# First half of the value projection moved from key tile 7 to key tile 6 in a fused attention kernel

## The chip, the cores and the metric

The kernel runs on one NeuronCore of a Trainium2 chip. The metric is the device time of one execution in microseconds (us); lower is better. Engines are named as in the profile: PE (TensorE matmuls), PEld (TensorE weight loads), DVE (VectorE), ACT (ScalarE), POOL (GpSimd), SP (SyncE, which issues all DMAs here).

## The reference, cut to what matters

One transformer block on x of shape (4, 1024, 256): self attention with 16 heads of 64, cross attention to a context of 77 rows, and a feed-forward layer, each behind a layer norm whose gain and shift come from a condition vector. The change lies in the self attention:

```python
def _attn(xq, ctx, wq, wkv, wo, bo):
    q = _heads(xq @ wq)
    k, v = jnp.split(ctx @ wkv, 2, axis=-1)
    ...
    sim = jnp.einsum('bhnd,bhmd->bhnm', q, k) * DH ** (-0.5)
    a = jax.nn.softmax(sim, axis=-1)
    o = jnp.einsum('bhnm,bhmd->bhnd', a, v)
    ...
    return o @ wo + bo
attn_in = _adaln(x, cond, ln1_w, ln1_b, g1_w, g1_b, b1_w, b1_b)
x = _attn(attn_in, attn_in, sa_wq, sa_wkv, sa_wo, sa_bo) + x
```

## The kernel before, in words

The self attention (`self_attention`) works through 32 head pairs: 4 batches times 8 pairs of heads, counted by g from 0 to G - 1 = 31. The 1024 keys of a pair are cut into 8 key tiles (kt) of 128. The 1024 queries are handled in two halves (c = 0 and 1), and the two heads of a pair lie in the two halves of the 128 partitions. Products of 16-bit high and low parts stand in for 32-bit ones, so each projection has three terms.

The order of the work on every engine is written out by hand: each engine has its own loop over g and kt, and semaphores join them. Engines work strictly in that order. In step (g, kt) PE does, in turn:

- `differences(j, kt)` (L460) for the next pair j = g + 1, into `ps_t`, whose halves are the two turning buffers `turn[0]` and `turn[1]`. ACT's `rises` (L701) takes the positive part of it.
- `scores(g, kt, c)` (L483), twelve matmuls into `ps_s[0]` and `ps_s[1]`. For kt = 0 the order is c = 1, then c = 0, and c = 0 also waits for the evacuated values (`s_v_r`).
- `bases(j, kt)` (L467), again into `ps_t`, after ACT's rise. DVE's `maxima` (L895) then writes one column of row maxima per head to `mx`.
- `shift()` (L490), which subtracts the row maxima in `m_line` from the scores. For kt = 0 it waits for the DMA that brings that line (`s_line`). ACT's `exponentials` (L713) follow, one for each c.
- `values(g, kt - 1, 0)` (L505), an extra piece of work if the step has one, and `values(g, kt - 1, 1)`.

The extra pieces are hung on certain key tiles, and those on the turning buffers have to wait until DVE has read the maxima there (`maxima_free`). K projections of pair g + 2 stand in key tiles 0 and 1, Q projections of pair g + 3 in 3 and 5 (L55, evacuated by ACT at L687), and the second half of the value projection (`V_SECOND`, L43, evacuated at L692) in key tile 2. The column sums of the previous pair (`totals`, L515, evacuated at L732) stand in key tile 0. Every projection into a turning buffer is followed, at the head of the next step, by a wait for its evacuation.

At the end of key tile 7 stands the turn to the next pair: PE transposes `mx` into `turn[1]` (L660), waits for the exponential of c = 0, and computes the first half of the value projection of pair j into the left half of `ps_s[0]` (`project_v(j, 0)`, L43). Meanwhile ACT copies the transposed maxima to `m_rows` (`row`, L705) and SP sends them to `m_line` by DMA (L302). Then ACT evacuates the values (`evacuate_v`, L692). The next step, key tile 0 of the next pair, opens with waits, the last of which is this one, because `differences` overwrites `turn[1]`:

```python
if kt == 0:
    pe.wait_ge(s_kd, j + 1)
    ...
    pe.wait_ge(s_mt_r, g + 1)
```

Some pairs carry more. For each of the six later layer norms (`NORMS`, with the pair it begins in), ACT normalises rows (`normalise`, L745) in key tiles 4 to 7 of the pair after the first and 0 to 3 of the one after that. In the second and third pair after the first, PE transposes the normalised rows (`transposes`, L540) in key tiles 4 and 6 (`NORM_AT`), ACT scales them (`norm_affine`, L752) and rounds them (`norm_high`, L757), and DVE makes the low half (`norm_low`, L982). In pairs 9, 17 and 25 (`late_norm`) PE writes the eight output row tiles of the batch that is done (`output`, L524 and L55; `Y_AT`), and DVE adds the residual (L928). DVE further sums the exponentials (`add_probs`, L908) in every step and makes the low half of the keys (`low`, L887), in key tile 7 for the K side of pair g + 2.

Of the kernel before, what the change touches and what calls it, by code (L numbers as in the profile page):

```python
# [14 lines left out]
B, N, D = 4, 1024, 256  # L15
# [44 lines left out]
def self_attention(nc, consts, x_src, x_dst, cond, norm, weights, bo, xT, wq, wk, wv, wo, shared, context, following):  # L60
# [9 lines left out]
    K_AT, Q_AT = (0, 1), (3, 5)  # L70
    V_FIRST, V_SECOND = NK - 1, 2
    Y_AT = {1: (0,), 2: (1,), 3: (2,), 4: (3, 4), 5: (5,), 6: (6, 7)}
    NORMS = {1: (0, 1), 2: (5, 2), 3: (10, 3), 4: (16, 0), 5: (21, 1), 6: (28, 2)}
    CROSS_NORMS = 4
    NORM_AT = {(2, 4): 0, (2, 6): 1, (3, 4): 2, (3, 6): 3}
    STATS_AT = {0: (0, 1, 2), 1: (3,), 3: (4, 5), 5: (6, 7)}
    STEPS = 10
    with ExitStack() as ctx:
# [153 lines left out]
        def v_bank(j, c):  # L232
            return turn[0] if c or j == 0 else ps_s[0][:, 0:HALF]

# [37 lines left out]
        def y_bank(b, t):  # L272
            if b < B - 1:
                return turn[0 if t in (3, 6) else 1][:, 0:D]
            places = [ps_s[0][:, 0:D], ps_s[0][:, HALF:HALF + D], ps_s[1][:, 0:D], ps_s[1][:, HALF:HALF + D],
                      turn[0][:, 0:D], turn[1][:, 0:D], ps_o[:, 0:D], ps_o[:, HALF:HALF + D]]
            return places[t]
# [5 lines left out]
        def score_count(g, kt, c):  # L283
            return 2 * NK * g + 2 * kt + order(kt).index(c) + 1
# [153 lines left out]
        def _(pe):  # L438
# [149 lines left out]
            for g in range(G):  # L588
                j = g + 1
                for kt in range(NK):  # L590
                    if j < G:
                        if kt == 0:
                            pe.wait_ge(s_kd, j + 1)
                            pe.wait_ge(s_hi[0], j + 1)
                            pe.wait_ge(s_hi[1], j + 1)
                            pe.wait_ge(s_mt_r, g + 1)
                            if g == 0:
                                pe.wait_ge(s_v_r, 1)
                        else:
                            maxima_free(j, kt - 1, 2)  # L600
                            if kt - 1 in K_AT and g + 2 < G:
                                pe.wait_ge(s_kq_r[0], 2 * (g + 2) + K_AT.index(kt - 1) + 1)
                            if kt - 1 in Q_AT and g + 3 < G:
                                pe.wait_ge(s_kq_r[1], 2 * (g + 3) + Q_AT.index(kt - 1) + 1)
                            if kt - 1 == V_SECOND and g >= 0:
                                pe.wait_ge(s_v_r, 2 * g + 2)
                            if kt == 1 and g >= 1:
                                pe.wait_ge(s_sum_r, g)
                            if norm_bank(g, kt - 1) is not None:
                                u, n = norm_bank(g, kt - 1)  # L610
                                pe.wait_ge(s_nxn, 4 * u + n + 1)
                            for b, t in y_tiles(g, kt - 1):
                                pe.wait_ge(s_yr, TT * b + t + 1)
                        differences(j, kt)
# [13 lines left out]
                    if last[0] >= 0:  # L628
                        values(*last, 0)
                    if j < G and (kt in K_AT + Q_AT + (V_SECOND,) or norm_bank(g, kt) is not None):  # L630
                        maxima_free(j, kt, 1)
# [4 lines left out]
                    if kt == V_SECOND and g >= 0:  # L636
                        project_v(g, 1)
                    if norm_bank(g, kt) is not None:
                        u, n = norm_bank(g, kt)
# [16 lines left out]
                    if last[0] >= 0:  # L656
                        values(*last, 1)
                    if kt == V_FIRST and j < G:
                        maxima_free(j, kt, 2)
                        pe.transpose(turn[1][0:2 * TT, 0:P], mx[:, j % 2, :], ident[:, :]).then_inc(s_mt, 1)  # L660
                        pe.wait_ge(s_p, score_count(g, kt, 0))
                        project_v(j, 0)
            for c in range(2):
# [18 lines left out]
        def _(act):  # L682
# [121 lines left out]
            for g in range(G):  # L804
                j = g + 1
                for kt in range(NK):
# [27 lines left out]
                    if kt == V_SECOND and g >= 0:  # L834
                        evacuate_v(g, 1)
                    if kt == 0 and g >= 1:
                        evacuate_sums(g - 1)
                        evacuate_o(g - 1, 1)
# [8 lines left out]
                    if norm_bank(g, kt) is not None:  # L847
                        norm_affine(*norm_bank(g, kt))
                        norm_high(*norm_bank(g, kt))
                    if kt == V_FIRST and j < G:  # L850
                        row(j)
                        evacuate_v(j, 0)
                    if g == G - 2 and kt in (1, 3):
# [16 lines left out]
        def _(dve):  # L870
# [205 lines left out]
            for g in range(G):  # L1076
                j = g + 1
                for kt in range(NK):
                    if j < G:
                        maxima(j, kt)  # L1080
                    if kt == 6 and norm_bank(g, 4) is not None:
                        norm_low(*norm_bank(g, 4))
# [29 lines left out]
                    if kt == 6 and g >= 1 and not late_norm(g):  # L1112
                        low_output(g - 1, 0)
                    if kt == 7 and g + 2 < G:
                        low(g + 2, 0)
# [11 lines left out]
                    if norm_of(g, 1) is not None and kt == 3:  # L1127
                        newton_step(norm_of(g, 1))
                    if kt == 0 and g >= 1 and norm_bank(g - 1, 6) is not None:
                        norm_low(*norm_bank(g - 1, 6))  # L1130
                    if g == G - 2 and kt in (2, 4):
# [1175 lines left out]
```

## Time and profile before

| what | us |
|---|---|
| runs | 2149.64, 2154.3, 2148.78; median 2149.64 |
| the profiled execution, its own time | 2151.02 |
| its span from first to last instruction | 2149.2 |
| mean granted TensorE clock, share of full speed | 0.981 |

A timeline lists instructions in order of time with their start, length, engine, source line and tiles; neighbours of a kind are merged into one line with a count. In brackets stands how long the engine was idle before it, and what ended that. Matmuls are pipelined: the length shown for one is longer than the distance to the next.

### The profile page before, as it was taken

Reading aid. Unit: us, or ns where it says so; the run is one execution under the profiler, and the core shown is the slowest. Engines: PE = TensorE matmul, PEld = TensorE weight load, DVE = VectorE, ACT = ScalarE, POOL = GpSimd, SP = SyncE. Lnnn points to the kernel's source line nnn. Section 1 sums busy time; section 2 is a strip of 40 time slices with the busy share of each in tenths; the row PEclk is TensorE's granted clock in tenths of the full one; section 3 lists DMA queues with packets and bytes.
Section 4 is the critical chain, followed back from the end, with each engine's and each line's share of the span. In section 5 each row is a group of like instructions: output and inputs, shape, how many; then the busy total and the mean of one; then the engine's idle time right before and its main releaser. Section 6 shows DMA issues by size and latency. Waiting matters only on the chain. (4 is left out here: it accounts for less than half of the span.)

```text
span 2149.2 us, 43063 instructions
## 1 busy us (share of the span) xinstructions
PE 2040.5 (95%) x17544; PEld 934.3 (43%) x17544; DVE 1751.1 (81%) x2720; ACT 1429.1 (66%) x1844; POOL 18.1 (1%) x16
## 2 busy tenths in 40 slices
PE   4799999999999999999999999999988999979999
PEld 2233333345333334533333453333633455446676
DVE  6899899986999998699989779987588888754754
ACT  4588778774787777577787657786457666652452
POOL 3000000000000000000000000000000000000000
PEclk8899999999999999999999999999998999999999
DMA  6010111011111111111011012021332344333111
GB/s 204 30 40 31 60 40 41 31 60 41 61 41 40 51 41 41 41 60 60 31 41 41 31 51 80 31 56 35 102 113 91 106 145 141 105 101 109 40 40 40
DMA packets 100347, 136.62 MB, mean 64 GB/s; under 512 B 34533, under 2 KB 73399, under 8 KB 100151
## 3 DMA queue, kind: packets, MB, share of 16 engines
q1 hardware_dynamic: 100151, 133.88, 18.9%
q8 instruction: 139, 2.28, 0.4%
q14 instruction: 57, 0.47, 0.1%
HBM read 68.34 MB, written 13.11 MB: 38 GB/s over the span
## 5 line engine op out<-in xcount | busy, mean ns | idle before, releaser
L713 ACT ACTIVATE sa_probs<-sa_ps_s 128x1024 f32<-128x1024 f32 x512 | 496.1, 1022 | 130.9 <-PE sa_ps_s L490 130.8
L505 PE MATMUL sa_ps_o<-sa_probs,sa_v_pair 128*64 128x512 f32 x2048 | 531.0, 609 | 1.4 <-DVE sa_mx L895 1.4
L908 DVE TENSOR_TENSOR sa_acc<-sa_acc,sa_probs 128x1024 f32<-128x1024 f32 x384 | 452.7, 1220 | 19.8 <-ACT sa_probs L713 11.9
L895 DVE CUSTOM_DVE_ANT_0 sa_rise<-sa_ps_t,sa_rise 128x512 f32<-128x512 f32 x504 | 327.3, 687 | 121.8 <-PE sa_ps_t L467 121.6
L483 PE MATMUL sa_ps_s<-scores_or_weights 64*128 64x512 f16 x3072 | 374.8, 376 | 1.5 <-ACT raw_or_keys L687 1.5
L701 ACT ACTIVATE sa_rise<-sa_ps_t 128x1024 f32<-128x1024 f32 x252 | 257.4, 1021 | 140.8 <-PE sa_ps_t L460 139.4
L483 PEld LDWEIGHTS sa_ps_s<-scores_or_weights 64*128 64x128 f16 x3072 | 151.9, 94 | 156.1 <-ACT sa_v_pair L692 6.8
L505 PEld LDWEIGHTS sa_ps_o<-sa_probs,sa_v_pair 128*64 128x64 f32 x2048 | 115.8, 135 | 149.8 <-issue 126.8
L460 PE MATMUL sa_ps_t<-sa_kd,scores_or_weights 64*128 64x512 f16 x504 | 99.3, 389 | 19.3 <-ACT scores_or_weights L697 6.8
L460 PEld LDWEIGHTS sa_ps_t<-sa_kd,scores_or_weights 64*128 64x128 f16 x504 | 25.2, 93 | 201.1 <-issue 163.1
L467 PE MATMUL sa_ps_t<-scores_or_weights 64*128 64x512 f16 x504 | 98.1, 385 | 11.3 <-ACT sa_rise L701 11.2
L490 PE MATMUL sa_ps_s<-sa_m_line,sa_m_ones 32*128 32x512 f16 x1024 | 101.3, 385 | 0.0
L687 ACT ACTIVATE raw_or_keys<-sa_ps_t 128x512 f32<-128x512 f32 x118 | 71.1, 603 | 32.6 <-PE sa_ps_t L55 32.6
L908 DVE TENSOR_TENSOR sa_acc<-sa_probs 128x1024 f32<-128x1024 f32 x64 | 75.5, 1221 | 9.1 <-ACT sa_probs L713 6.4
L873 DVE TENSOR_TENSOR raw_or_keys<-raw_or_keys,ropeC 128x1024 f32<-128x1024 f32 x64 | 78.0, 1219 | 5.3 <-DMA sa_swp<-raw_or_keys 5.3
L55 PE MATMUL ca_ps_t<-xT_hi,scores_or_weights 128*64 128x512 f16 x512 | 80.6, 396 | 0.0
L2113 ACT ACTIVATE ff_hid<-ff_ps_h,ff_b_col 128x1024 f32<-128x1024 f32 x32 | 35.6, 1113 | 62.3 <-PE ff_ps_h L43 61.4
L878 DVE TENSOR_TENSOR raw_or_keys<-raw_or_keys,sa_swp 128x1024 f32<-128x1024 f32 x62 | 75.7, 1221 | 1.1
L874 DVE TENSOR_TENSOR sa_swp<-sa_swp,ropeS 128x1024 f32<-128x1024 f32 x62 | 75.5, 1218 | 0.0
L55 PE MATMUL ca_ps_t<-scores_or_weights,ca_o_hi 128*64 128x256 f16 x800 | 74.7, 284 | 0.0
L887 DVE TENSOR_TENSOR scores_or_weights<-raw_or_keys,scores_or_weights 128x1024 f16<-128x1024 f32 x62 | 73.8, 1191 | 0.4 <-ACT scores_or_weights L697 0.4
L697 ACT ACTIVATE scores_or_weights<-raw_or_keys 128x1024 f16<-128x1024 f32 x64 | 67.4, 1054 | 9.8 <-DVE raw_or_keys L878 9.8
(338 smaller groups left out, 3656.2 us busy)
## 6 DMA issues: line engine op xcount, KB each, us to landing
sa_swp<-raw_or_keys SPq DMA_DIRECT2D x124, 256.0 KB, 2.4
sa_inv<-sa_scratch SPq DMA_DIRECT2D x128, 128.0 KB, 2.9
ca_swp<-raw_or_keys SPq DMA_DIRECT2D x64, 256.0 KB, 2.4
ca_inv<-ca_scratch SPq DMA_DIRECT2D x64, 256.0 KB, 3.9
sa_xs<-in_x SPq DMA_DIRECT2D x4, 1024.0 KB, 5.7
sa_xr<-in_x SPq DMA_DIRECT2D x4, 1024.0 KB, 6.8
x_after_cross<-scores_or_weights SPq DMA_DIRECT2D x32, 128.0 KB, 2.2
ff_xr<-x_after_cross SPq DMA_DIRECT2D x4, 1024.0 KB, 6.3
```

The source lines that it names most:

```text
L55: ins = pe.matmul(out[part], lhs[a][lhs_at(k)][:, part], rhs[b][rhs_at(k)], start=(start and i == 0), stop=(stop and i == len(terms) - 1))
L460: ins = pe.matmul(max_banks(j, t)[:, half(x)], hi[rows(x), j % 3, 1, t * P:(t + 1) * P], kd[rows(x), j % 2, :], start=True, stop=True)
L467: ins = pe.matmul(max_banks(j, t)[:, half(x)], hi[rows(x), j % 3, 1, t * P:(t + 1) * P], hi[rows(x), j % 3, 0, 0:HALF], start=True, stop=True)
L483: pe.matmul(ps_s[c][:, half(x)], k[rows(x), s, 0, ks], q[rows(x), s, 1, half(c)], start=(n == 0), stop=False)
L490: ins = pe.matmul(ps_s[c][:, half(x)], m_ones[quarter, :], m_line[quarter, :], start=False, stop=True)
L505: ins = pe.matmul(ps_o[rows(x), half(c)], v_pair[:, kt, rows(x)], probs[:, kt % 2, c, half(x)], start=(kt == 0), stop=(kt == NK - 1))
L701: act.activation(rise_of(j, t), max_banks(j, t), ACT.Relu).then_inc(s_rise, 1)
L713: act.activation(probs[:, kt % 2, c, :], ps_s[c][:, :], ACT.Exp, scale=float(DH) ** -0.5).then_inc(s_p, 1)
L873: dve.tensor_tensor(raw[:, i, :], raw[:, i, :], ropeC[:, :], ALU.mult).then_inc(s_mul[i], 1)
L878: dve.tensor_tensor(raw[:, i, :], raw[:, i, :], swapped(j, i)[:, :], ALU.add).then_inc(s_rot[i], 1)
L895: dve.tensor_tensor_reduce(out=larger, in0=max_banks(j, t)[:, half(x)], in1=larger, scale=1.0, scalar=-3.0e38, op0=ALU.add, op1=ALU.max, a ...
L908: dve.tensor_tensor(acc[:, c, :], before, probs[:, kt % 2, c, :], ALU.add).then_inc(s_acc[c], 1)
```

## The change

The first half of the value projection moves from the end of key tile 7 to key tile 6, between the two `values` of that step, and goes to `turn[0]` in place of `ps_s[0]`; ACT evacuates it there, and PE waits for that at the head of key tile 7. The transpose of the maxima stays at the end of key tile 7, as do `row` and its DMA. What stood on `turn[0]` in key tile 6 makes room: the second and fourth of each layer norm's transposes go to key tile 7, the last output row tile goes to key tile 7, and the buffers of output tiles 6 and 7 change places. At the head of the next key tile 0, PE now also waits for the evacuation of those two. On DVE, the low half of the K side goes from key tile 7 to 6, and a layer norm's low half from key tile 6 to 5.

```diff
-    V_FIRST, V_SECOND = NK - 1, 2
-    Y_AT = {1: (0,), 2: (1,), 3: (2,), 4: (3, 4), 5: (5,), 6: (6, 7)}
+    V_FIRST, V_SECOND = NK - 2, 2
+    Y_AT = {1: (0,), 2: (1,), 3: (2,), 4: (3, 4), 5: (5,), 6: (6,), 7: (7,)}
...
-    NORM_AT = {(2, 4): 0, (2, 6): 1, (3, 4): 2, (3, 6): 3}
+    NORM_AT = {(2, 4): 0, (2, 7): 1, (3, 4): 2, (3, 7): 3}
...
         def v_bank(j, c):
-            return turn[0] if c or j == 0 else ps_s[0][:, 0:HALF]
+            return turn[0]
...
-                return turn[0 if t in (3, 6) else 1][:, 0:D]
+                return turn[0 if t in (3, 7) else 1][:, 0:D]
...
                             pe.wait_ge(s_mt_r, g + 1)
+                            if norm_bank(g - 1, NK - 1) is not None:
+                                u, n = norm_bank(g - 1, NK - 1)
+                                pe.wait_ge(s_nxn, 4 * u + n + 1)
+                            for b, t in y_tiles(g - 1, NK - 1):
+                                pe.wait_ge(s_yr, TT * b + t + 1)
...
+                            if kt - 1 == V_FIRST:
+                                pe.wait_ge(s_v_r, 2 * j + 1)
...
-                    if j < G and (kt in K_AT + Q_AT + (V_SECOND,) or norm_bank(g, kt) is not None):
+                    if j < G and (kt in K_AT + Q_AT + (V_FIRST, V_SECOND) or norm_bank(g, kt) is not None):
                         maxima_free(j, kt, 1)
...
+                    if kt == V_FIRST and j < G:
+                        project_v(j, 0)
...
-                    if kt == V_FIRST and j < G:
+                    if kt == NK - 1 and j < G:
                         maxima_free(j, kt, 2)
                         pe.transpose(turn[1][0:2 * TT, 0:P], mx[:, j % 2, :], ident[:, :]).then_inc(s_mt, 1)
-                        pe.wait_ge(s_p, score_count(g, kt, 0))
-                        project_v(j, 0)
...
+                    if kt == V_FIRST and j < G:
+                        evacuate_v(j, 0)
...
-                    if kt == V_FIRST and j < G:
+                    if kt == NK - 1 and j < G:
                         row(j)
-                        evacuate_v(j, 0)
...
-                    if kt == 6 and norm_bank(g, 4) is not None:
+                    if kt == 5 and norm_bank(g, 4) is not None:
                         norm_low(*norm_bank(g, 4))
...
-                    if kt == 7 and g + 2 < G:
+                    if kt == 6 and g + 2 < G:
                         low(g + 2, 0)
...
-                    if kt == 0 and g >= 1 and norm_bank(g - 1, 6) is not None:
-                        norm_low(*norm_bank(g - 1, 6))
+                    if kt == 0 and g >= 1 and norm_bank(g - 1, 7) is not None:
+                        norm_low(*norm_bank(g - 1, 7))
```

## Rows read from the trace of the kernel before

**Rows 1.** The page, part 1: busy us, share of the span, instructions of each engine.
```profile
PE 2040.5 (95%) x17544; PEld 934.3 (43%) x17544; DVE 1751.1 (81%) x2720; ACT 1429.1 (66%) x1844; POOL 18.1 (1%) x16
```

**Rows 2.** Windows from one `differences` to the next: stretch, us, busy us per engine, clock, DMA.
```profile
780.98:785.01 4.03, 4.03 (x30) 1.28 (x29) 3.65 (x8) 3.29 (x4) 0.00 (x0) 1.00 0.34 136
785.01:790.59 5.58, 5.58 (x56) 2.72 (x55) 5.58 (x9) 3.94 (x6) 0.00 (x0) 1.00 0.00 0
...
760.68:766.31 5.63, 5.63 (x55) 2.54 (x54) 5.23 (x10) 3.56 (x4) 0.00 (x0) 1.00 0.37 140
```

**Rows 3.** Timeline of PE, key tile 7 of a plain pair and the next key tile 0.
```profile
786.53 0.38 PE L467 MATMUL sa_ps_t<-scores_or_weights 64*128 64x512 f16 x2
...
789.04 0.28 PE L660 MATMUL sa_ps_t<-sa_ident,sa_mx 128*16 128x128 f32 x1
...
792.26 0.39 PE L467 MATMUL sa_ps_t<-scores_or_weights 64*128 64x512 f16 x2
792.58 0.40 PE L490 MATMUL sa_ps_s<-sa_m_line,sa_m_ones 32*128 32x512 f16 x4
```

**Rows 4.** Timeline of ACT, the same pair, key tiles 2 and 7.
```profile
765.40 0.60 ACT L692 ACTIVATE sa_v_pair<-sa_ps_t 128x512 f32<-128x512 f32 x1 [0.50 <-PE sa_ps_t L43]
...
787.29 1.94 ACT L713 ACTIVATE sa_probs<-sa_ps_s 128x1024 f32<-128x1024 f32 x2 [0.31 <-PE sa_ps_s L490]
789.35 0.27 ACT L705 ACTIVATE sa_m_rows<-sa_ps_t 16x128 f16<-16x128 f32 x1
790.69 0.60 ACT L692 ACTIVATE sa_v_pair<-sa_ps_s 128x512 f32<-128x512 f32 x1 [1.07 <-PE sa_ps_s L43]
```

**Rows 5.** The waits of the whole span: us in total, times, longest us.
```profile
PEld sa_ps_s L483 <- ACT sa_v_pair L692: 6.8, 31, 0.4
```

**Rows 6.** Timeline of PE and ACT, layer norm pair with normalisation in key tile 7.
```profile
612.27 0.39 PE L460 MATMUL sa_ps_t<-sa_kd,scores_or_weights 64*128 64x512 f16 x2
...
616.43 0.28 PE L660 MATMUL sa_ps_t<-sa_ident,sa_mx 128*16 128x128 f32 x1
...
617.98 0.39 PE L460 MATMUL sa_ps_t<-sa_kd,scores_or_weights 64*128 64x512 f16 x2
...
617.00 0.25 ACT L705 ACTIVATE sa_m_rows<-sa_ps_t 16x128 f16<-16x128 f32 x1
```

**Rows 7.** Timeline of PE and ACT, key tile 6 of a pair with layer norm transposes.
```profile
651.89 0.39 PE L460 MATMUL sa_ps_t<-sa_kd,scores_or_weights 64*128 64x512 f16 x2
...
656.92 0.39 PE L460 MATMUL sa_ps_t<-sa_kd,scores_or_weights 64*128 64x512 f16 x2 [0.20 <-ACT sa_xn L752]
...
655.99 0.78 ACT L752 ACTIVATE sa_xn<-sa_ps_t,bet,gam 128x512 f32<-128x512 f32 x1
656.81 0.63 ACT L757 ACTIVATE xT_hi<-sa_xn 128x512 f16<-128x512 f32 x1
657.35 1.02 ACT L701 ACTIVATE sa_rise<-sa_ps_t 128x1024 f32<-128x1024 f32 x1
```

**Rows 8.** Timeline of PE, key tile 6 of pair 9: starts of output row tiles.
```profile
520.74 0.30 PE L524 MATMUL sa_ps_t<-sa_bo_rows,sa_two_ones 128*64 128x256 f16 x2
...
523.49 0.28 PE L524 MATMUL sa_ps_t<-sa_bo_rows,sa_two_ones 128*64 128x256 f16 x2
```

**Rows 9.** Timeline of DVE, the plain pair, from key tile 7 into key tile 0.
```profile
790.69 1.22 DVE L887 TENSOR_TENSOR scores_or_weights<-raw_or_keys,scores_or_weights 128x1024 f16<-128x1024 f32 x1
...
792.69 0.69 DVE L895 CUSTOM_DVE_ANT_0 sa_rise<-sa_ps_t,sa_rise 128x512 f32<-128x512 f32 x1 [0.18 <-PE sa_ps_t L467]
```

**Rows 10.** DMA issues (count, KB each, median us to landing), and SP's timeline at that turn.
```profile
sa_swp<-raw_or_keys SPq DMA_DIRECT2D x124, 256.0 KB, 2.4
...
sa_few<-sa_sums SPq DMA_DIRECT2D x128, 2.0 KB, 1.8
...
sa_m_line<-sa_m_rows SPq DMA_DIRECT2D x32, 4.0 KB
...
789.64 0.62 SPq L302 DMA_DIRECT2D sa_m_line<-sa_m_rows  x1
```

## The prediction

> **What bounds the kernel now.** I began with the page's busy shares: PE shows 95%, DVE 81%, ACT 66% [rows 1]. Then I read the timeline of PE and cut it into steps, from one `differences` to the next, because the change only moves work between the steps of key tiles 6, 7 and 0. The windows over these steps show the pattern [rows 2]. A step of a plain pair without an extra piece (key tile 6) takes 4.03 us. The step of key tile 7 with the turn to the next pair takes 5.58. Key tile 2, which carries the other half of the same value projection, takes 5.63. PE is busy from end to end in all three. I take the length of a step, not the busy share, as the measure of what PE's order costs, since every piece hung on a step lengthens it.
>
> The second thing to see is what lies at the turn. The transpose of the maxima starts at 789.04 [rows 3]. ACT's copy of it starts at 789.35, when that 0.28 us transpose is through, and ends at 789.62 [rows 4]. ACT's two exponentials had ended before (787.29 + 1.94 = 789.23), so they do not set this. The next `differences` starts only at 790.59 [rows 2], because PE is in the value projection until then. The wait for ACT's copy (`s_mt_r`) is therefore already over when PE gets to it. The projection costs PE time there, but it also covers that chain.
>
> **The change part by part.** I count one plain pair first, then the others. All sums are against the profiled execution.
>
> Key tile 6 gains the projection. The nearest row is key tile 2, which has the same 24 matmuls, the same buffer and the same place between two `values`: 5.63 against 4.03, so +1.60 [rows 2]. The lower end is what the projection costs at the turn: 790.59 - 789.04 = 1.55 with the maxima's transpose in it [rows 2, 3], so about 1.40 without. I take 1.60, the same place. ACT's evacuation (0.60) now stands in key tile 6 ahead of ACT's rise of key tile 7, and PE waits for it before that step's `differences`. In key tile 2 the same evacuation ends at 766.00, and `differences` starts at 766.31 [rows 2, 4]. It is hidden by `values`, with 0.3 to spare; without that cover the step would be up to 0.6 longer.
>
> Key tile 7 loses the projection, and now nothing stands between the transpose and the wait. From the transpose's start, ACT's copy ends 789.62 - 789.04 = 0.58 later. PE's reaction comes on top. Where PE's `differences` waited for ACT in the same place, ACT ended at 655.99 + 0.78 = 656.77 and PE went on at 656.92 [rows 7], so 0.15; I take that, with 0 as the lower end. The step up to the transpose is 789.04 - 785.01 = 4.03 [rows 2, 3]. The new step is 4.03 + 0.58 + 0.15 = 4.76, against 5.58: -0.82.
>
> Key tile 0 loses a small stall. Its scores for c = 0 waited for the values, 31 times and 6.8 us in all [rows 5], and ACT's rise stood behind the evacuation. From `differences` to `bases` it took 792.26 - 790.59 = 1.67, where the step before took 786.53 - 785.01 = 1.52 [rows 2, 3]: -0.15. The lower end of this gain is 0.
>
> A plain pair: 1.60 - 0.82 - 0.15 = **+0.63**.
>
> In a pair with normalisation in key tile 7, that work stands ahead of ACT's copy. The copy ends at 617.25, 0.82 after the transpose [rows 6]. The new step is 4.03 + 0.82 + 0.15 = 5.00 against 617.98 - 612.27 = 5.71, so the pair is 1.60 - 0.71 - 0.15 = +0.74. I take 4.03 up to the transpose, although it shows 4.16 now, because the evacuation pushes the normalisation before it out of the rise's way.
>
> In a pair with layer norm transposes, key tile 6 is 656.92 - 651.89 = 5.03 now [rows 7], and becomes 5.63. In key tile 7, ACT does `norm_affine` and `norm_high` between the exponentials and the copy. In key tile 6 the next ACT instruction comes at 657.35, which is 5.46 after the step's start [rows 7]. Adding the copy and PE's reaction gives 5.46 + 0.27 + 0.15 = 5.88 against 5.58. The pair is 0.60 + 0.30 - 0.15 = +0.75.
>
> In the pairs with output rows, one row tile costs 523.49 - 520.74 = 2.75 [rows 8] in either step, so moving it changes nothing: +0.63 as in a plain pair. Its residual on DVE is hidden by the second `values`.
>
> By the code's tables, of the 31 turns 12 are plain, 3 have output rows, 5 normalisation in key tile 7, and 11 transposes. The sum is 15 x 0.63 + 5 x 0.74 + 11 x 0.75 = 9.5 + 3.7 + 8.3 = +21.4 us.
>
> Moved at no cost: the low half of the keys on DVE. It takes 1.22 [rows 9]. DVE is busy 3.65 in key tile 6, so 4.87 there in a step of 5.63 [rows 2]. Behind it stand the maxima of key tile 7, which PE needs only at the transpose. DVE's wait of 0.18 at 792.69 [rows 9] shows that it keeps up with the turn now, and it has 1.22 less to do there afterwards. Without that cover it would add what it is late by, at most 1.22. The layer norm's low half only goes one step forward within DVE's order. In the last pair, the transposes in key tile 7 stand beside the wait for the last column sums. SP and POOL issue nothing new; SP's DMA of the maxima stands behind the same copy.
>
> That DMA loses cover, though. The copy ends at 789.62, the DMA is issued at 789.64 [rows 10], and `shift` of key tile 0 needs it at 792.58 [rows 3], so 2.96 after the copy. After the change, `shift` follows the copy by 0.15 + 1.52 + (792.58 - 792.26) = 1.99. The trace gives no landing time for this DMA of 4 KB. The nearest row, 2 KB from the same memory, lands after 1.8, the 256 KB ones after 2.4 [rows 10]. With 1.8 and PE's reaction it is ready at 0.02 + 1.8 + 0.15 = 1.97, just hidden, and I take 0. The ends are 0, as it cannot gain, and 2.96 - 1.99 = 0.97 a turn, as no row shows PE waiting for it now.
>
> The Trainium skill (DMA: Bandwidth & Descriptors, Anatomy of one DMA) puts a fixed 2.0 us on a DMA of any size. By that, `shift` would wait (0.02 + 2.0 + 0.15) - 1.99 = 0.18 a turn, and the sum would be an estimated 5.6 us more. No row here shows this DMA's landing, and the 1.8 beside it is lower, so I stay with the row.
>
> **Against the runs.** The profiled execution took 2151.02, which is its span of 2149.2 and 1.8 around it. The median of the three runs is 2149.64, 1.4 lower. The forecast goes from the median: 2149.64 + 21.4 = **2171.0 us**, +1.0%. A measurement of this kernel can tell about 0.3%, 6.4 us, from no change.
>
> **The rivals.** (a) The copy is hidden after all, and the step of key tile 7 shrinks by all that the projection took there, 5.58 to about 4.15. Then a turn costs 1.60 - 1.43 - 0.15 = 0.02, and the time is 2150. Against it, the transpose (0.28) and the copy (0.27) run one after the other, with nothing of PE beside them. Chance 6%.
>
> (b) Faster: PE is not the limit in key tile 6, and the projection disappears in its gaps. It decides where key tile 6 grows by less than the 0.82 + 0.15 = 0.97 that the turn gives back. If it were fully hidden, the time would be 2149.64 - 31 x 0.97 = 2120. For it speaks that weight loads fill only 43% [rows 1]; against it that the same projection lengthened key tile 2 by 1.60. Chance 5%. The Trainium skill (Perfetto Trace Analysis, Identifying the Most-Contended Engine) says that a matmul's busy share misjudges PE and that the share of weight loads is to be used. That is this rival, and the step lengths here speak against it.
>
> (c) Slower still: the line of maxima lands late, as the larger DMAs do. With 2.4, `shift` waits 0.02 + 2.4 + 0.15 - 1.99 = 0.58 a turn, 18 us more, 2189. It decides from 1.84 us of landing time. For it speaks how little is to spare, against it the 1.8. Chance 9%.
>
> That the change does not do what it says could show only in the freed bank: the scores of key tile 0 still begin with c = 1, so the freed `ps_s[0]` brings nothing but the 0.15.
>
> **How the numbers follow.** The forecast has 80%. Its low end: projection at 1.40 (-6), PE's reaction at 0 (-5); not both in full, so -10. Its high end: no gain in key tile 0 (+5) and the line late by a little (+6), so about +10. The range is 2161 to 2181; 6% and 5% lie below it with (a) and (b), most of (c) above. Slower by over 0.3%: the forecast less a small tail, and (c), 87%. Within 0.3%: (a) and that tail, 8%. Faster: 5%.
>
> **What would show it.** In the profile after, key tile 6 of a plain pair should take about 5.6, key tile 7 about 4.8, with the idle time of 0.5 to 0.6 before `differences` of key tile 0 put down to ACT's copy, and key tile 0 about 6.5. A turn with transposes should show ACT's `norm_high` ahead of the copy. It would be wrong if key tile 7 ends right behind the transpose, if key tile 6 grows by less than 1, or if PE waits at `shift` for the line.

## The result and the profile after

The change made the kernel slower by 49 us: 2199.53 us, median of four runs (2199.1 to 2204.81), against 2150.26, median of four (2148.78 to 2154.3). The ratio is 1.0233, with a 95% interval of 1.0215 to 1.0251. The direction is the forecast one, the size is not: 2171.0 was forecast, and the range ended at 2181.

The profiled execution is the slowest of the four, 2204.81, of which the span is 2202.9. Part of the growth of the span lies in the first pair, at the start of the kernel. That pair took between 45.9 and 49.2 us in the traces of this study (45.97 before, 49.23 after, 46.54 in a kernel that differs from the one after only in SP's order), and I leave its length out of the sums. The page, part 1, of the kernel after:

```profile
PE 2054.7 (93%) x17544; PEld 939.4 (43%) x17544; DVE 1753.0 (80%) x2720; ACT 1433.0 (65%) x1844; POOL 18.1 (1%) x16
```

PE's share fell from 95% to 93% [rows 1]. In microseconds, its busy time grew by only 14 (2054.7 - 2040.5) while the span grew by 53.7. So most of the loss is time in which PE waits; the 14 come up again with the clock below. The windows of the kernel after, from one `differences` to the next, tell where. The first three are key tiles 6, 7 and 0 of a plain turn, the last two key tile 7 of pair 9, which has output rows, and the key tile 0 behind it.

```profile
805.76:811.39 5.63, 5.63 (x55) 2.54 (x54) 5.25 (x10) 4.08 (x5) 0.00 (x0) 1.00 0.25 98
811.39:816.14 4.75, 4.30 (x31) 1.40 (x30) 4.53 (x9) 3.75 (x5) 0.00 (x0) 1.00 0.00 0
816.14:822.61 6.47, 6.47 (x48) 2.22 (x48) 6.04 (x9) 4.54 (x6) 0.00 (x0) 1.00 0.00 1
538.36:549.62 11.26, 7.22 (x82) 4.00 (x80) 4.96 (x9) 4.13 (x6) 0.00 (x0) 0.92 0.01 2
549.62:560.58 10.96, 10.07 (x48) 3.08 (x49) 6.85 (x12) 4.71 (x6) 0.00 (x0) 0.62 0.28 96
```

Against [rows 2], the plain turn does what was forecast: key tile 6 went from 4.03 to 5.63 and key tile 7 from 5.58 to 4.75. The turn of pair 9 does not. Its key tiles 7 and 0 took 5.58 and 6.64 before, and now take 11.26 and 10.96, at a mean granted clock of 0.62 in the second.

Cutting both traces at every `differences` gives the length of each pair. I worked these out from the starts of L460; each pair runs from its key tile 1 to the next key tile 0:

| kind of pair | before | after | difference | forecast |
|---|---|---|---|---|
| plain (12) | 42.03 | 42.64 | +0.61 | +0.63 |
| normalisation in key tile 7 (5) | 43.19 | 43.91 | +0.72 | +0.74 |
| layer norm transposes (11) | 44.52, 44.03 | 45.34, 44.85 | +0.82 | +0.75 |
| the same, pairs 3, 8, 19: more in key tile 0 | 6.63 | 8.61, 8.04, 7.99 instead of 6.47 | +2.14, +1.57, +1.52 | 0 |
| output rows, pairs 9, 17, 25 | 64.49, 64.50, 64.50 | 73.07, 71.19, 73.62 | +8.58, +6.69, +9.12 | +0.63 each |

Three pairs are counted with their kinds although their own lengths differ: pair 0 (plain) for the reason given, pair 29 (normalisation) with 41.23 and 42.05, and pair 30 (transposes), which has no next `differences` to end it.

The first three kinds make 7.3 + 3.6 + 9.0 = 19.9 us, the extra of pairs 3, 8 and 19 makes 5.2, and the pairs with output rows 24.4. That is 49.5, against 49.3 measured; the medians are not known to 0.2, so that part of the agreement is luck. Almost all that was missed lies in six turns.

The waits of PE in the kernel after (us in total, times, longest us) name three causes that the kernel before does not have at these places:

```profile
PE sa_ps_t L460 <- ACT sa_m_rows L712: 18.1, 27, 1.0
PE sa_ps_t L460 <- DVE sa_xr L936: 11.9, 3, 4.0
PE sa_ps_s L490 <- DMA sa_m_line<-sa_m_rows: 9.1, 7, 2.1
```

**The first** is the forecast one. The timeline of a plain turn, of PE and then of ACT:

```profile
815.42 0.28 PE L669 MATMUL sa_ps_t<-sa_ident,sa_mx 128*16 128x128 f32 x1
816.14 0.39 PE L460 MATMUL sa_ps_t<-sa_kd,scores_or_weights 64*128 64x512 f16 x2 [0.45 <-ACT sa_m_rows L712]
816.36 1.47 PE L483 MATMUL sa_ps_s<-scores_or_weights 64*128 64x512 f16 x12
...
815.73 0.27 ACT L712 ACTIVATE sa_m_rows<-sa_ps_t 16x128 f16<-16x128 f32 x1
```

ACT's copy ends at 816.00, 0.58 after the transpose began, and PE goes on 0.14 later. The working had 0.58 and 0.15.

**The second** belongs to the three pairs with output rows. The turn of pair 9, in the order PE, ACT, DVE, SP:

```profile
544.31 0.28 PE L55 MATMUL sa_ps_t<-sa_wo_lo,sa_o_hi 128*64 128x256 f16 x2
...
545.38 0.28 PE L669 MATMUL sa_ps_t<-sa_ident,sa_mx 128*16 128x128 f32 x1
549.62 0.61 PE L460 MATMUL sa_ps_t<-sa_kd,scores_or_weights 64*128 64x512 f16 x2 [3.97 <-DVE sa_xr L936]
550.00 2.79 PE L483 MATMUL sa_ps_s<-scores_or_weights 64*128 64x512 f16 x12
...
554.11 0.61 PE L490 MATMUL sa_ps_s<-sa_m_line,sa_m_ones 32*128 32x512 f16 x4 [0.89 <-DMA sa_m_line<-sa_m_rows]
...
544.69 1.15 ACT L733 ACTIVATE sa_o_hi<-sa_o_pair 128x512 f16<-128x512 f32 x2 [4.88 <-PE sa_ps_t L55]
545.74 1.92 ACT L720 ACTIVATE sa_probs<-sa_ps_s 128x1024 f32<-128x1024 f32 x2
547.55 0.25 ACT L712 ACTIVATE sa_m_rows<-sa_ps_t 16x128 f16<-16x128 f32 x1
...
546.78 2.36 DVE L916 TENSOR_TENSOR sa_acc<-sa_acc,sa_probs 128x1024 f32<-128x1024 f32 x2 [5.17 <-ACT sa_probs L720]
549.06 0.42 DVE L936 SCALAR_TENSOR_TENSOR sa_xr<-sa_ps_t,sa_xr 128x256 f32<-128x256 f32 x1
...
549.50 0.38 SPq L387 DMA_DIRECT2D x_after_self<-sa_xr  x1
549.92 0.62 SPq L302 DMA_DIRECT2D sa_m_line<-sa_m_rows  x1
```

Start at ACT. Its `high_output` (L733) rounds the output of the pair just done into `o_hi`, and the row tiles of the batch still read `o_hi`. In these pairs it therefore waits until all eight row tiles are through PE. The eighth was moved to key tile 7, so ACT stands still for 4.88 us until 544.69. Behind it in ACT's order stand the exponentials of key tile 7. DVE's sums need those, DVE's residual (L936) stands behind the sums in DVE's order, and it ends at 549.48. PE waits for it, because the row tile lies in the turning buffer: 3.97 us idle. Afterwards PE's twelve `scores` matmuls take 2.79 where a plain turn has 1.47.

The granted clock is the reason for that. It has two levels in these traces, 1.00 (2.4 GHz) and 0.50 (1.2 GHz), and 0.62 is a mean of both. While PE stands idle it falls to 0.50, and it stays there for the first 8.3 us of key tile 0. The windows of that stretch, and of the key tiles 0 behind pairs 17 and 25:

```profile
549.62:557.95 8.33, 7.44 (x32) 2.61 (x34) 5.71 (x9) 3.52 (x4) 0.00 (x0) 0.50 0.37 126
927.37:936.44 9.07, 7.83 (x48) 2.65 (x50) 5.86 (x9) 4.54 (x6) 0.00 (x0) 0.85 0.35 118
1309.73:1321.24 11.51, 10.58 (x48) 3.15 (x49) 5.87 (x9) 4.72 (x6) 0.00 (x0) 0.59 0.27 91
```

PE is busy for 10.07, 7.83 and 10.58 us in these three steps, where a plain key tile 0 has 6.47. The lower clock thus takes 9.1 us of the 24.4, most of the 14 by which PE's busy time grew. The wait ahead was 3.97 all three times, but the lower level ended sooner behind pair 17, which is why that pair lost about 2 us less than the other two.

**The third** lies on SP's queue. When all rows of a batch are done, SP stores 1 MB (L387); it waits for the residual of the eighth tile, so it is now issued at 549.50, just ahead of the line of maxima at 549.92. At the turn after pair 3, it is a load that stands there (L333). It waits until PE has done the transposes of the layer norm before, and the last set of these was moved to key tile 7 as well. SP, then PE, of the kernel after:

```profile
255.84 0.39 SPq L333 DMA_DIRECT2D sa_xs<-in_x  x1
257.71 0.62 SPq L302 DMA_DIRECT2D sa_m_line<-sa_m_rows  x1
...
257.94 0.39 PE L460 MATMUL sa_ps_t<-sa_kd,scores_or_weights 64*128 64x512 f16 x2 [0.92 <-ACT sa_m_rows L712]
...
261.92 0.39 PE L490 MATMUL sa_ps_s<-sa_m_line,sa_m_ones 32*128 32x512 f16 x4 [2.07 <-DMA sa_m_line<-sa_m_rows]
```

SP in the kernel before, at the same two places:

```profile
245.73 0.39 SPq L333 DMA_DIRECT2D sa_xs<-in_x  x1
251.54 0.62 SPq L302 DMA_DIRECT2D sa_m_line<-sa_m_rows  x1
...
526.88 0.38 SPq L387 DMA_DIRECT2D x_after_self<-sa_xr  x1
531.81 0.62 SPq L302 DMA_DIRECT2D sa_m_line<-sa_m_rows  x1
```

There, the large transfer has 4.9 to 5.8 us before the small one is issued. After the change it has 0.4 to 1.9. The line of 4 KB then reaches PE 261.92 - 257.71 = 4.21 us after its issue.

### The profile page after: what moved, and what is told of

Read it like the earlier page. It is cut to its first block and busy times, and to the rows that moved or that the text cites. A ratio compares the mean times of both kernels' runs of the same rounds, so it can differ in the third digit from the quotient of the medians.

```text
span 2202.9 us, 43080 instructions
## 1 busy us (share of the span) xinstructions
PE 2054.7 (93%) x17544; PEld 939.4 (43%) x17544; DVE 1753.0 (80%) x2720; ACT 1433.0 (65%) x1844; POOL 18.1 (1%) x16
## 5 line engine op out<-in xcount | busy, mean ns | idle before, releaser
L505 PE MATMUL sa_ps_o<-sa_probs,sa_v_pair 128*64 128x512 f32 x2048 | 540.3, 613 | 1.4 <-DVE sa_mx L903 1.4
L460 PE MATMUL sa_ps_t<-sa_kd,scores_or_weights 64*128 64x512 f16 x504 | 100.0, 391 | 47.2 <-ACT sa_m_rows L712 18.1
L460 PEld LDWEIGHTS sa_ps_t<-sa_kd,scores_or_weights 64*128 64x128 f16 x504 | 25.7, 93 | 230.9 <-issue 210.1
L43 PE MATMUL sa_ps_t<-sa_wv_hi,xT_hi 128*128 128x128 f16 x512 | 90.9, 222 | 0.9 <-DVE sa_mx L903 0.9
L43 PE MATMUL sa_ps_t<-sa_wv_hi,xT_lo 128*128 128x128 f16 x512 | 90.2, 220 | 0.0
L43 PE MATMUL sa_ps_t<-sa_wv_lo,xT_hi 128*128 128x128 f16 x512 | 90.2, 220 | 0.0
```

The lines of the kernel that those rows point to most:

```text
L43: ins = pe.matmul(out, lhs[a][lhs_at(k)], rhs[b][rhs_at(k)], start=(start and i == 0), stop=(stop and i == len(terms) - 1))
L460: ins = pe.matmul(max_banks(j, t)[:, half(x)], hi[rows(x), j % 3, 1, t * P:(t + 1) * P], kd[rows(x), j % 2, :], start=True, stop=True)
L505: ins = pe.matmul(ps_o[rows(x), half(c)], v_pair[:, kt, rows(x)], probs[:, kt % 2, c, half(x)], start=(kt == 0), stop=(kt == NK - 1))
```

## The experiments

The theory was that three costs add up: the turn (about 20 us), ACT's wait for the eighth row tile (with the lower clock behind it), and the line behind the large transfer. The rival was that the row tiles and transposes are harmless, and that the projection in key tile 6 itself delays ACT and DVE in those turns.

**The line first.** The kernel after, with SP's issue of the line ahead of the store and the load:

```diff
+                if g + 1 < G:
+                    line(g + 1)
                 if g >= PAIRS and g % PAIRS == 1:
...
                     load_norm(norm_of(g, -2))
-                if g + 1 < G:
-                    line(g + 1)
```

> The change with one edit: SP issues the DMA of the maxima line ahead of the store of finished output rows and the load for the next layer norm, instead of behind them. Queue theory (a 1 MB transfer moved just ahead of that small DMA makes it land after 3.6 to 4.2 us instead of 1.7): the stalls at shift of key tile 0 after pairs 3, 8 and 19 (2.1 + 1.6 + 1.5) and the one in the three pairs with output rows go, together about 9 us, 2190 us against 2199.5. Rival (the excess comes from DVE's moved low halves or from the TensorE clock alone): no change, 2199.

Measured: 2186.52, ratio to the kernel before 1.0167 (1.0147 to 1.0186). The windows of pair 9's key tile 7 and of the key tile 0 behind it, then PE's wait for the line:

```profile
532.21:543.47 11.26, 7.22 (x82) 4.00 (x80) 4.95 (x9) 4.13 (x6) 0.00 (x0) 0.91 0.01 3
543.47:552.23 8.76, 8.76 (x48) 2.72 (x48) 6.14 (x11) 4.65 (x6) 0.00 (x0) 0.72 0.35 120
```
```profile
PE sa_ps_s L490 <- DMA sa_m_line<-sa_m_rows: 1.0, 1, 1.0
```

The waits for the line fell from 9.1 to 1.0 us, and key tile 0 after pairs 3, 8 and 19 is back at 6.47: the order on SP's queue was the cause there. The 1.0 that is left stands at the last turn, where no `differences` come ahead of `shift`. Key tile 7 of pair 9 is unchanged, with its wait for DVE's residual. Its key tile 0 is still 8.76 with PE busy throughout, where a plain one takes 6.47. With no wait left in it, these 2.3 us go with the clock: it stands at 0.50 for the first 4.9 us of the step, and half of that is 2.4.

**The rounding late.** The kernel after, with ACT's `high_output` behind the exponentials in those pairs:

```diff
-                    if kt == 7 and g >= 1:
-                        if late_norm(g):
-                            high_output(g - 1, 0)
+                    if kt == 7 and g >= 1 and not late_norm(g):
                         high_output(g - 1, 1)
                     if g >= 0:
                         for c in order(kt):
                             exponentials(g, kt, c)
+                    if kt == 7 and g >= 1 and late_norm(g):
+                        for c in range(2):
+                            high_output(g - 1, c)
```

> The change with one edit: in the pairs with output rows ACT rounds the finished outputs of the previous pair (which waits for the last output row tile) behind the exponentials of key tile 7 instead of ahead of them. Chain theory (last row tile, rounding, exponentials, sums of exponentials, residual, then PE): key tile 7 of pairs 9, 17 and 25 falls from 11.26 to about 7.9, and PE's clock stays up in the next key tile 0, but the maxima line still stands behind the store; about 15 us off, 2184. Rival (the extra time of these pairs is the output tile's own cost or the store): 2197 to 2199.

Measured: 2181.63, ratio 1.015 (1.0125 to 1.0175). The same two windows, then PE's wait for the line:

```profile
535.70:543.59 7.89, 7.22 (x81) 4.01 (x80) 5.80 (x10) 4.27 (x6) 0.00 (x0) 1.00 0.04 13
543.59:551.70 8.11, 6.54 (x48) 2.22 (x48) 6.19 (x11) 4.54 (x6) 0.00 (x0) 1.00 0.35 120
```
```profile
PE sa_ps_s L490 <- DMA sa_m_line<-sa_m_rows: 10.5, 8, 2.1
```

Key tile 7 falls from 11.26 to 7.89, and the clock stays at 1.00 in both windows: ACT's wait was the head of that chain. Key tile 0 keeps 8.11 - 6.47 = 1.64 of the line's wait.

**Both.** The two edits together.

> Both edits on top of the change. If the two theories hold and do not overlap with the turn, what is left is the turn alone: plain pairs 42.64, pairs with output rows 66 to 67, 2172 us, 22 us over the kernel before. Rival: over 2185.

Measured: 2173.85, ratio 1.0109 (1.009 to 1.0127). The same two windows:

```profile
533.99:541.88 7.89, 7.23 (x81) 4.01 (x80) 5.80 (x10) 4.27 (x6) 0.00 (x0) 1.00 0.01 3
541.88:548.36 6.48, 6.48 (x50) 2.21 (x50) 4.90 (x8) 4.54 (x6) 0.00 (x0) 1.00 0.48 162
```

Pairs 9, 17 and 25 take 65.21, 65.70 and 65.21, so +0.7, +1.2 and +0.7 is left of +8.6, +6.7 and +9.1. All other pairs are as in the table, without the extra of pairs 3, 8 and 19. The sum by pairs, 19.9 + 2.6 = 22.5, meets the measured 2173.85 - 2151.45 = 22.4, closer than the four runs, which lie 5.5 apart, would let one expect. This is the cost that the forecast described.

With these kernels pair 9's +8.58 can be split: 0.72 with both edits, 11.26 - 7.89 = 3.37 for the chain in key tile 7, and 10.96 - 6.47 = 4.49 in key tile 0, of which 2.3 remains with the line first, and 2.2 goes with it. Only 0.89 of these 2.2 is PE's wait for the line; the rest goes with the lower clock, which lasted longer there. Over pairs 9, 17 and 25 together, the rounding late takes 17.4 us away, the line first 6.0, and both 21.8, so the costs do add up, nearly.

**The move without the rest.** The projection stays in key tile 6, but transposes and row tiles go back there, behind it, each with the wait that the shared buffer needs:

```diff
-    Y_AT = {1: (0,), 2: (1,), 3: (2,), 4: (3, 4), 5: (5,), 6: (6,), 7: (7,)}
+    Y_AT = {1: (0,), 2: (1,), 3: (2,), 4: (3, 4), 5: (5,), 6: (6, 7)}
...
-    NORM_AT = {(2, 4): 0, (2, 7): 1, (3, 4): 2, (3, 7): 3}
+    NORM_AT = {(2, 4): 0, (2, 6): 1, (3, 4): 2, (3, 6): 3}
...
-            return (ps_o[:, 0:HALF], ps_o[:, HALF:N], turn[0], turn[1])[n] if u == 0 else turn[0]
+            return (ps_o[:, 0:HALF], ps_o[:, HALF:N], turn[0], turn[1])[n] if u == 0 else turn[n % 2]
...
+                        if t == 7:
+                            pe.wait_ge(s_v_r, 2 * j + 1)
...
```

> The first half of the value projection in key tile 6 as in the change, but layer norm transposes and both last output row tiles stay in key tile 6 (the transposes in the other turning buffer, the last row tile behind the evacuation of the values). Turn theory: 31 turns at about 0.62 each and nothing else, 2170 us. Rival (moving the projection costs all of the 49 us, whatever stands beside it): 2199; rival (the moved tiles cost it all): 2150.

Measured: 2162.91, ratio 1.0061 (1.0044 to 1.0078), 7 us below what I expected, and far from both rivals. Key tile 6 of a pair with transposes:

```profile
658.37:664.50 6.13, 6.13 (x58) 2.94 (x57) 6.05 (x10) 4.86 (x7) 0.00 (x0) 1.00 0.23 88
```

Plain pairs still take 42.64, pairs 9, 17 and 25 64.80, 65.13 and 64.80. The pairs with transposes take 44.65 and 44.15, only +0.13. A set of transposes behind the projection adds 6.13 - 5.63 = 0.5, where in a key tile 6 of its own it added 5.03 - 4.03 = 1.0. That was not expected, and it is where most of the 7 us come from. Of the difference of 0.5, 0.20 is a wait: in the step of its own PE stands idle for 0.20 at the end, until ACT has evacuated the set [rows 7], and behind the projection it does not. The rest is open.

**The rest without the move.** The kernel before, with all other parts of the change (transposes and row tile in key tile 7, the low halves on DVE one step earlier), the projection at the turn:

```diff
-    Y_AT = {1: (0,), 2: (1,), 3: (2,), 4: (3, 4), 5: (5,), 6: (6, 7)}
+    Y_AT = {1: (0,), 2: (1,), 3: (2,), 4: (3, 4), 5: (5,), 6: (6,), 7: (7,)}
...
-    NORM_AT = {(2, 4): 0, (2, 6): 1, (3, 4): 2, (3, 6): 3}
+    NORM_AT = {(2, 4): 0, (2, 7): 1, (3, 4): 2, (3, 7): 3}
...
-                    if kt == 7 and g + 2 < G:
+                    if kt == 6 and g + 2 < G:
                         low(g + 2, 0)
...
```

> The kernel before with everything of the change but the projection: second and fourth layer norm transposes and the last output row tile in key tile 7, the low halves one key tile earlier, the projection still at the turn in the score buffer. Theory of three parts: no cost at plain turns (42.03 a pair); pairs 9, 17 and 25 still suffer the chain through the rounding and the late line, about 6 us each; the loads after pairs 3, 8 and 19 about 1 each: 2169 us. Rival (all cost hangs on the projection's place): 2150.

Measured: 2191.31, ratio 1.0175 (1.0154 to 1.0196), 22 us above what I expected. A wait of PE at the transpose of the maxima shows why:

```profile
PE sa_ps_t L665 <- DVE sa_mx L900: 10.3, 16, 1.1
```

DVE's low half, 1.22 us, now stands in a key tile 6 of 4.03 us with no projection to cover it, and the maxima come late. The next two kernels take this apart.

**The low half alone.** The kernel before, with only the last of these edits.

> The kernel before with one edit of the change: DVE makes the low half of the keys in key tile 6 instead of 7, and nothing else moves. Cover theory (this 1.2 us was free in the change only because the projection lengthened key tile 6): the maxima of key tile 7 come late, PE waits for them at their transpose, key tile 7 of a plain pair goes from 5.58 to about 6.24, as it did in e5_room_only, about 20 us in all, 2171 us. Rival (what lengthened e5_room_only's plain turns was something else in it): 2151.

Measured: 2162.6, ratio 1.005 (1.0033 to 1.0066). Key tile 7 of a plain pair, and PE's transpose of the maxima in it:

```profile
789.65:795.89 6.24, 5.65 (x56) 2.72 (x55) 6.24 (x10) 3.94 (x6) 0.00 (x0) 1.00 0.00 0
```
```profile
794.34 0.28 PE L660 MATMUL sa_ps_t<-sa_ident,sa_mx 128*16 128x128 f32 x1 [0.59 <-DVE sa_mx L895]
```

The step takes 6.24 instead of 5.58 (6.42 in some plain pairs), with DVE busy from end to end. The edit costs 11 us and not the 20 that I expected, because the pairs with transposes or row tiles have a longer key tile 6 here, which covers it: their key tile 7 takes 5.66 and 5.58.

**The tiles without the low half.** The kernel with the rest alone, the low half back in key tile 7:

```diff
-                    if kt == 6 and g + 2 < G:
+                    if kt == 7 and g + 2 < G:
                         low(g + 2, 0)
```

> e5_room_only with the low half of the keys back in key tile 7: the projection at the turn, the second and fourth layer norm transposes and the last output row tile in key tile 7. Plain turns back at 5.58; left are the chain and the late line in pairs 9, 17 and 25 and the loads after pairs 3, 8 and 19: 15 to 20 us over before, about 2170. Rival (the room costs nothing without the projection's move): 2151.

Measured: 2170.76, ratio 1.009 (1.0075 to 1.0105). Pair 9's key tile 7 and the key tile 0 behind it:

```profile
525.84:537.10 11.26, 8.74 (x105) 5.34 (x104) 4.15 (x8) 4.73 (x7) 0.00 (x0) 1.00 0.01 2
537.10:547.62 10.52, 7.89 (x48) 2.54 (x50) 7.90 (x13) 4.71 (x6) 0.00 (x0) 0.84 0.30 100
```

With the projection where it was, key tile 7 is again 11.26 long, and pairs 9, 17 and 25 take 71.33, 71.59 and 71.64. Key tile 0 after pairs 3, 8 and 19 takes 8.36, 7.64 and 7.76 instead of 6.63, while plain pairs take their 42.03. This decides against the rival: both missed costs come with the moved row tiles and transposes, and the projection need not move for them. The 19.0 here and the 10.8 of the low half alone make 29.8 of the 37.1 that the kernel with both lost. Most of the rest lies in the pairs with transposes: with both, their key tile 6 is short again and covers nothing, and their key tile 7 takes 7.22 against 6.31 here.

**Another bank for the maxima.** The kernel with both edits, and the transposed maxima in the freed bank `ps_s[0]`, so that only the scores of c = 0 wait for ACT's copy:

```diff
+        def row_bank(j):
+            return (ps_s[0] if j else turn[1])[0:2 * TT, 0:P]
...
                 elif c == 0:
                     pe.wait_ge(s_v_r, 2 * g + 1)
+                    pe.wait_ge(s_mt_r, g + 1)
...
-                            pe.wait_ge(s_mt_r, g + 1)
+                            if g == 0:
+                                pe.wait_ge(s_mt_r, g + 1)
...
+                        pe.wait_ge(s_p, score_count(g, kt, 0))
+                        pe.transpose(row_bank(j), mx[:, j % 2, :], ident[:, :]).then_inc(s_mt, 1)
...
```

> The change with both edits of e3_both, and the maxima are transposed into the score buffer that the projection has left, so that the differences of the next key tile 0 no longer wait for ACT's copy; only the scores of c = 0 do, which come 0.9 us later. Turn theory (the bare copy chain is what the turn costs): key tile 7 of a plain pair falls from 4.75 to about 4.15, 2150 us, level with the kernel before. Rival (the projection's place in key tile 6 is the cost, the wait only shows it): no change against e3_both.

Measured: 2164.93, ratio 1.0053 (1.0034 to 1.0071), where 2150 was expected. Key tile 7 and key tile 0 of a plain turn, PE's wait for the line, and that turn's timeline (ACT, SP, PE):

```profile
794.82:799.05 4.23, 4.23 (x31) 1.36 (x30) 4.01 (x8) 3.49 (x4) 0.00 (x0) 1.00 0.00 0
799.05:805.82 6.77, 6.54 (x51) 2.16 (x50) 6.74 (x11) 4.81 (x7) 0.00 (x0) 1.00 0.00 1
```
```profile
PE sa_ps_s L494 <- DMA sa_m_line<-sa_m_rows: 10.5, 31, 0.8
```
```profile
799.16 0.27 ACT L718 ACTIVATE sa_m_rows<-sa_ps_s 16x128 f16<-16x128 f32 x1
...
799.45 0.62 SPq L305 DMA_DIRECT2D sa_m_line<-sa_m_rows  x1
...
801.18 0.40 PE L494 MATMUL sa_ps_s<-sa_m_line,sa_m_ones 32*128 32x512 f16 x4 [0.23 <-DMA sa_m_line<-sa_m_rows]
```

Key tile 7 shrinks from 4.75 to 4.23, but key tile 0 grows from 6.47 to 6.77. With the wait for the copy gone, the next thing late is the line, at every one of the 31 turns. It reaches PE 801.18 - 799.45 = 1.73 us after its issue. So neither side came out: the wait for the copy did cost something, but only part of what its end saved is kept, because the next wait stands just behind it.

**Transposes beside other projections.** Since a set was cheap behind the value projection, I put all four sets of the kernel before behind projections in key tiles 5, 1, 3 and 5, in the other turning buffer and with the waits that this needs:

```diff
-    NORM_AT = {(2, 4): 0, (2, 6): 1, (3, 4): 2, (3, 6): 3}
+    NORM_AT = {(2, 5): 0, (3, 1): 1, (3, 3): 2, (3, 5): 3}
...
```

> The kernel before with the layer norm transposes hung on steps that already carry a projection (key tile 5 of one pair, 1, 3 and 5 of the next), in the other turning buffer. In e4_move_only a set of transposes behind the value projection lengthened its step by 0.5 us, alone in a step by 1.0. If that holds beside the K and Q projections too: 22 sets by 0.5, 11 us less than the kernel before, 2140. Rival (the 0.5 belongs to key tile 6, or DVE, which makes a low half more in these steps, comes late): 2151 or above.

Measured: 2151.35 (10 runs) against 2151.78 (13 runs), ratio 1.0002 (0.9992 to 1.0012): no difference, where 2140 was expected. Two of the steps that carry a set:

```profile
668.02:674.27 6.25, 6.25 (x47) 2.32 (x45) 4.52 (x9) 5.76 (x8) 0.00 (x0) 1.00 0.03 4
679.90:686.36 6.46, 6.26 (x46) 2.22 (x45) 6.46 (x10) 4.43 (x6) 0.00 (x0) 1.00 0.05 19
```

These are key tiles 1 and 3, which take 5.49 and 5.32 without a set: it costs 0.76 and 1.14 there, not 0.5. In the second, DVE is busy throughout, and PE waits 0.20 for it. The other layer norms gained 0.3 us each, 1.4 in all; pair 30 lost more than that, with 34.96 against 32.13 from its key tile 1 to its key tile 7. No kernel of this study beats the one before.

## Why the prediction was right and wrong

**Right: the turn.** The direction and the first three rows of the table rest on the working's own steps. Key tile 6 cost +1.60, as key tile 2 said [rows 2]; key tile 7 gave back 0.83 where 0.82 was forecast; key tile 0 gave 0.16 where 0.15 was forecast. Those pairs make 19.9 us, against 7.6 + 3.7 + 8.3 = 19.6 in the sum. In the pairs with transposes, ACT's later copy moved the end of key tile 7 to 5.96, with 5.88 forecast. Rivals (a) and (b) fell by their own signs: PE waits for the copy, and key tile 6 grew by far more than 0.97. The rule that stood beside (b), of the Trainium skill (Perfetto Trace Analysis, Identifying the Most-Contended Engine), does not agree with these traces as far as weight loads go: their share stayed at 43%, and each inserted piece lengthened its step. The share of peak arithmetic, which the same rule names beside it, was not worked out here.

**Right: the cover.** The low half on DVE was put at nothing, with the projection as its cover, at most 1.22 without it. The two kernels without that cover show 6.24 - 5.58 = 0.66 at a plain turn (0.84 at some), and with it PE does not wait there.

**Right, and close: the line.** It was called just hidden, at 1.8 us of landing time. With another bank for the maxima it shows itself: 1.73 from issue to PE. At plain turns of the kernel after, PE does not wait for it. The fixed 2.0 us of the Trainium skill (DMA: Bandwidth & Descriptors, Anatomy of one DMA) is above this measurement; that section gives it for DMAs which GpSimd issues, and this one is issued by SP. Rival (c) is true at six turns only, and for a cause that it did not name. Its threshold is a slip: from its own terms it is 1.99 - 0.02 - 0.15 = 1.82, not 1.84. At the last turn PE waits 1.01 though the line takes its ordinary 1.73: no `differences` and `bases` stand ahead of `shift` there, and the one sum for all 31 turns left that out.

**Wrong: "moving it changes nothing".** This is the step on the pairs with output rows: PE's time for a row tile is the same in either step, and that was all I priced. The step also claimed that the residual on DVE is hidden. Neither follows the eighth tile to those who wait for it. ACT's `high_output` waits for `s_y` because it overwrites what the tile reads, and ACT's exponentials stand behind it. The term was +0.63 for each of three pairs and measured +8.58, +6.69 and +9.12. This is 22.5 us of the 28 by which the forecast was short. Of it, 9.1 is the lower clock that followed PE's idle time, for which the working had no term. With the rounding late alone, 17.4 of it go.

**Wrong: "SP and POOL issue nothing new".** It is true that no DMA was added. But two old ones wait for what was moved: the store for the eighth residual, the load for the last set of transposes. They now go out just ahead of the line, instead of 5 us before. This is 5.2 us at pairs 3, 8 and 19, and 6.0 within the 22.5 just named, by the kernel with the line first (2.19, 0.35 and 3.48 in pairs 9, 17 and 25). Both steps have the same fault: the waits named were those that the diff adds, not those that already hung on what the diff moves. With both repaired by order alone, the time is 2173.85, inside the range.

**What stays open.** Why a set of transposes costs 0.5 behind the value projection and 0.76 to 1.14 elsewhere, beyond the waits of 0.20 named above; and 0.4 of the 7.89 that key tile 7 takes in the kernel with both edits (4.76 forecast for the turn, 2.75 for the tile). No run shows why the lower clock lasted 8.3 us into one key tile 0 and under 3 us into another with the same wait ahead, nor why a small transfer lands later behind a large one; only that issuing it first ends this. The 0.15 for the maxima's transpose behind the low end of 1.40 stands in no row; with the other bank, key tile 7 is 4.23 - 4.03 = 0.20 longer than up to its transpose, and no bound rested on it alone.

## What to carry to other kernels

When a change moves a piece of work later, list everybody who waits for it, also those that the diff does not touch: the engine that wants to overwrite its input, and the queue whose next transfer it releases. For each, ask what stands behind that wait in the same order; here the two answers cost more than the change itself. And when work is moved for free under a cover, write down what the cover is: without it the same edit cost 11 us.

## What was not expected of the hardware

A transfer of 4 KB reached PE 1.73 us after its issue when no large one had been issued just before it, and 4.21 us after it when a transfer of 1 MB had been issued 1.87 us earlier from the same engine (255.84 and 257.71). After PE had stood idle for 3.97 us, the granted clock was at 0.50, the lower level, and twelve matmuls took 2.79 instead of 1.47; idle times of 0.45 at every plain turn left it at 1.00. The same 3.97 us of idle time did not cost the same each time: the mean clock of the step behind it was 0.62, 0.85 and 0.59.
